# Expert results sent to a token-order table slot by slot, rotary tables made once and kept, first input tile and last output split, and the program's order laid anew

## What is computed

```python
xn = _layernorm(x, axis=-1)
x = x + _L0_attn_ref(xn, ...) + _L0_ffn_ref(xn, ...)
# attention: 16 query heads, 4 key/value heads, head size 128, causal
q = _layernorm(q, q_norm_w, q_norm_b); k = _layernorm(k, k_norm_w, k_norm_b)
q = _rope(q, cos, sin);                k = _rope(k, cos, sin)
attn = softmax(where(causal, q @ k.T / sqrt(D), -inf))
out = ((attn @ v) * sigmoid(gate)) @ w_o.T
# experts: 8, the two best of each token
top_vals, top_idx = jax.lax.top_k(x_flat @ w_router, 2)
probs = jax.nn.softmax(top_vals, axis=-1)
y = square(relu(x @ w_fc[e])) @ w_proj[e]        # for each expert e
out = sum over the token's two experts of probs * y
```

## Time and profile before

| | us |
|---|---|
| median of 3 runs | 1561.65 |
| lowest and highest | 1560.73, 1561.84 |
| profiled execution, its own time | 1561.02 |
| profiled execution, span of its instructions | 1559.2 |
| PE busy | 1508.5 (97%) |
| DVE busy | 1310.9 (84%) |
| ACT busy | 1154.7 (74%) |
| POOL busy | 523.9 (34%) |
| mean granted TensorE clock | 0.996 |

### The profile page before, as it was taken

The page is one execution under the profiler, slowest core; times in us unless marked ns, Lnnn a source line. Parts: engine busy times, 40 slices in busy tenths (PEclk is TensorE's granted clock), DMA queues, the critical chain, the costliest instruction groups (busy, mean ns, idle before and its releaser), DMA issues.

```text
span 1559.2 us, 29914 instructions
## 1 busy us (share of the span) xinstructions
PE 1508.5 (97%) x10589; PEld 1380.0 (89%) x10589; DVE 1310.9 (84%) x3011; ACT 1154.7 (74%) x3013; POOL 523.9 (34%) x726
## 2 busy tenths in 40 slices
PE   4999999999899999999999999999999999999998
PEld 3788999999899999999898999999998998899998
DVE  7999888787898888788789888887779988888875
ACT  3777777777778787787778777777777776776775
POOL 5544434320553222121046331221105535343200
PEclk9999999999999999999999999999999999999999
DMA  4400010001111000101211000110111101102000
GB/s 139 142 5 21 21 42 23 21 28 50 45 33 30 32 30 29 32 26 39 66 45 40 25 25 11 47 31 30 28 46 45 33 13 31 30 20 66 16 8 8
DMA packets 46646, 56.65 MB, mean 36 GB/s; under 512 B 4576, under 2 KB 43232, under 8 KB 46304
## 3 DMA queue, kind: packets, MB, share of 16 engines
q1 hardware_dynamic: 43424, 46.34, 9.5%
q0 software_dynamic: 3072, 8.39, 1.7%
HBM read 42.40 MB, written 18.35 MB: 39 GB/s over the span
## 4 chain that ended last, share of the span: by engine, by line
PE 74%; DVE 17%; ACT 5%; issue 2%; POOL 1%; DMA 1%; SPq 0%; DVEq 0%; ACTq 0%; POOLq 0%
PE bank L1286 39%; PE o_bank L1286 19%; PE pt_bank L1361 12%; DVE pT_lo L1219 3%; DVE neg_chunk_max L1205 2%; DVE t_same L1169 2%; DVE bank L1202 2%; PE bank L1339 1%; PE bank L1382 1%; DVE t_same L1165 1%; ACT probs L920 1%; DVE sumsq L1137 1%; DVE t_same L1153 1%; ACT gate L930 1%; ACT pT_hi L939 1%
## 5 line engine op out<-in xcount | busy, mean ns | idle before, releaser
L920 ACT ACTIVATE probs<-bank,neg_max 128x512 f32<-128x512 f32 (+3 forms) x640 | 399.8, 634 | 91.7 <-DVE neg_max L1212 57.6
L1219 DVE TENSOR_TENSOR pT_lo<-pt_bank,pT_hi 128x512 fp32r<-128x512 f32 (+1 forms) x576 | 368.7, 654 | 100.7 <-ACT pT_hi L939 96.8
L939 ACT ACTIVATE pT_hi<-pt_bank 128x512 fp32r<-128x512 f32 (+1 forms) x576 | 325.8, 578 | 131.3 <-PE pt_bank L1361 81.6
L1286 PE MATMUL o_bank<-pT_hi,v_hi 128*128 128x256 f32 x1088 | 333.7, 307 | 2.9 <-DVE pT_lo L1219 1.9
L1361 PE MATMUL pt_bank<-ident_f,probs 128*128 128x128 f32 x2176 | 315.2, 273 | 10.5 <-DVE pT_lo L1219 10.0
L785 POOL TENSOR_TENSOR t_swap<-qk_raw,table_swap 128x256 f32<-128x256 f32 (+1 forms) x256 | 135.4, 560 | 561.9 <-ACT t_same L889 560.9
L1286 PE MATMUL o_bank<-pT_hi,v_lo 128*128 128x256 f32 x1088 | 307.3, 282 | 0.0
L1286 PE MATMUL o_bank<-pT_lo,v_hi 128*128 128x256 f32 x1088 | 306.5, 282 | 0.0
L1205 DVE TENSOR_REDUCE neg_chunk_max<-bank 128x1 f32<-128x512 f32 (+1 forms) x384 | 244.8, 650 | 49.2 <-PE bank L1286 48.1
L1361 PEld LDWEIGHTS pt_bank<-ident_f,probs 128*128 128x128 f32 x2176 | 252.2, 140 | 36.0 <-DVE pT_lo L1219 13.5
L1286 PE MATMUL bank<-kT_hi,qT_hi 128*128 128x512 f32 (+3 forms) x640 | 244.0, 381 | 2.7 <-ACT probs L920 2.3
(11 more groups left out here) (163 smaller groups left out, 2974.6 us busy)
## 6 DMA issues: line engine op xcount, KB each, us to landing
rows<-xs SPq DMA_DIRECT2D x23, 256.0 KB, 2.7
expert_raw<-in_w_fc SPq DMA_DIRECT2D x23, 256.0 KB, 3.0
expert_raw<-in_w_proj SPq DMA_DIRECT2D x23, 256.0 KB, 2.7
yb<-rows SPq DMA_DIRECT2D x23, 256.0 KB, 2.1
xs<-in_x SPq DMA_DIRECT2D x11, 512.0 KB, 4.9
w_raw<-in_w_in SPq DMA_DIRECT2D x7, 640.0 KB, 4.3
angles<-in_cos_sin SPq DMA_DIRECT2D x64, 64.0 KB, 1.9
acc<-in_x SPq DMA_DIRECT2D x4, 512.0 KB, 8.3
```

The costliest lines, as they stand in the source:

```text
L920: act.activation(probs[:, u, h % 2, first:first + width], bank("scores", g, t, h, c)[:, 0:width], ACT.Exp, bias=neg_max[:, u, h % 2:h % 2 ...
L939: act.activation(pT_hi[:, n % PT_RING, 0:width], pt_bank[n % 2][:, 0:width], ACT.Copy)\
L1219: dve.tensor_tensor(pT_lo[:, n % PT_RING, 0:width], pt_bank[n % 2][:, 0:width], pT_hi[:, n % PT_RING, 0:width].bitcast(F32), ALU.subtract) ...
L1286: ins = pe.matmul(out_ap, s, m, start=(start and done == 1), stop=(stop and done == last))
```

## The change

Seven things are done together.

1. **Scatter of results.** Each row of `xs` gets two more columns, the number of the token's pair (2·token + j), scattered with the row; unused rows carry the number of a spare row. After `y_take`, POOL sends the slot's rows with two indirect DMAs (`y_place`) to the table `y_of` in token order, to the row numbers that DVE has made integers (`ids`). The second waits for the first, and the next `xs_load` waits for both. `y_store` and the 32 gathers are gone; after the last slot, SP reads `y_of` with 16 plain loads (`y_load`), through four buffers, and `comb` waits for these.
2. **Kept tables.** POOL makes the rotary tables only in group 0 (16 times, not 64). SP stores each to memory (384 KB) and loads it again in groups 1 to 3, alternately over `made_tables` and over the norm rows' place (48 loads of 384 KB); 48 loads of 64 KB of angles go.
3. **First tile.** x comes in parts of 1, 3, 4, 4 and 4 tiles; Q, K, V and the gate of tile 0 wait for the first alone. The router's products of tile 0 to 3 come later.
4. **Loads at the start.** The norm weights come as one load of rows already broadcast on the host's side; the router's weights are laid out by partition.
5. **Last tile.** Its `og`, `og_hi`, `og_lo` and `OUT` are done in two halves of two heads. `GT` and the first half of `OUT` stand ahead of the last products with V.
6. **Scatter order.** First all of j = 0, then all of j = 1.
7. **Order.** `BEGIN` and `DUE` have new numbers, with three shifts for each tile, and some costs of the plan are changed.

The core of the diff (the tables of numbers cut to a line):

```diff
-BEGIN = [26.59, 41.38, 29.62, 36.09, 25.65, 50.81, 47.59, 46.92, 64.18, 72.49, 75.23, 89.37, 102.35, 116.24,
+BEGIN = [4.36, 32.9, 50.6, 39.96, 9.9, 26.58, 41.54, 17.1, 36.65, 69.46, 20.35, 39.2, 39.91, 55.0, 87.1, 99.04,
...
+X_PARTS = ((0, 1), (1, 4), (4, 8), (8, 12), (12, 16))
...
+                if t >= 2:
+                    add("sp angles", ("angle_load", g, t), 0.45, [old(t2, "tables")], b0 + DUE["rope"] - 15, 64)
+                table = ("tables", g, t)
...
+                add("sp tables", ("table_store", t), 0.45, [table], 0, 384)
+            else:
+                table = ("table_load", g, t)
...
-            add("pool rope", ("swap", g, t), 2.0, [("kv_take", g, t), old(t1, "rope_b")], b0 + DUE["rope"])
+            add("pool rope", ("swap", g, t), 2.0, [("kv_take", g, t), table, old(t1, "rope_b")], b0 + DUE["rope"])
...
+                for p in range(HG // 2):
+                    add("dve out", ("og", g, t, p), 0.33, [("GT", g, t), ("o_take", g, t, p)], b2 + DUE["og"])
+                    add("act og", ("og_hi", g, t, p), 0.3, [("og", g, t, p), old(t1, "OUT")], b2 + DUE["og"])
+                    add("dve og", ("og_lo", g, t, p), 0.33, [("og_hi", g, t, p)], b2 + DUE["og"])
...
-        add("sp moe", ("y_store", m), 0.45, [("y_take", m)], at + 8, 256)
+        add("dve ids", ("ids", m), 0.1, [("xs_load", m)], at)
+        for k in range(2):
+            add("pool y", ("y_place", m, k), 1.27, [("y_take", m), ("ids", m), ("y_place", m, 0) if k else None], at + 8 + 6 * k, 2.0)
...
+        add("sp y", ("y_load", t), 0.45, [("y_place", NSLOT - 1, 1), ("comb", t - 4) if t >= 4 else None], at + 20 + 3 * t, 256)
...
-                    for i, v in enumerate((q_w, k_w)):
-                        sp.dma_start(ln_w[:, i, :], v.partition_broadcast(P)).then_inc(tables_in, 16)
-                    for i, v in enumerate((q_b, k_b)):
-                        sp.dma_start(ln_b[:, i, :], v.partition_broadcast(P)).then_inc(tables_in, 16)
+                    sp.dma_start(norm_rows[:, 0:2], norm_in).then_inc(tables_in, 16)
...
+                elif kind == "table_load":
+                    g, t = a
+                    n = g * T + t
+                    w.wait_ge(tables_kept, 16 * T)
...
+                elif kind == "y_place":
+                    m, k = a
+                    w.wait_ge(ids_done, m + 1)
+                    w.wait_ge(y_taken, m + 1)
+
+                    w.wait_ge(y_placed, 32 * m + 16 * k)
+                    pool.indirect_dma_start(y_of, bass.IndirectOffsetOnAxis(row_to[:, k:k + 1], 0), rows[:, k, 0:C], None)\
+                        .then_inc(y_placed, 16)
...
+                elif kind == "ids":
+                    m = a[0]
+                    w.wait_ge(xs_in, 16 * (m + 1))
+                    dve.tensor_copy(row_to[:], rows[:, :, C]).then_inc(ids_done, 1)
```

More of the change, by code:

```diff
@@ L157, in old @@
         return (kind, *tile, *rest) if tile is not None else None
-    for q in range(4):
-        add("sp", ("x_load", q), 0.5, [], 0, 512)
-        if q == 0:
+    for n, (first, last) in enumerate(X_PARTS):
+        add("sp", ("x_load", n), 0.5, [], 0, 128 * (last - first))
+        if n == 0:
             add("sp", ("ident_load",), 0.5, [], 0, 64)
@@ L199, in program_steps @@
         add("sp fill", ("fill", k), 0.45, [("tables", 0, 1 + k // 3)], 30 + k, 512)
-    for t in range(T):
-        for j in range(2):
-            add("pool sc", ("scatter", t, j), 1.27, [("route", ROUTE_PLACE), ("fill", FILLS - 1), ("turn_probs", *prob_steps[SCATTER_AT + SCATTER_EVERY * (2 * t + j)])],
-                DUE["scatter"], 2.0)
+    for j in range(2):
+        for t in range(T):
+            add("pool sc", ("scatter", t, j), 1.27, [("route", ROUTE_PLACE), ("fill", FILLS - 1), ("row_ids", j),
+                ("turn_probs", *prob_steps[SCATTER_AT + SCATTER_EVERY * (T * j + t)])], DUE["scatter"], 2.0)
+        add("act ids", ("row_ids", j), 0.25, [("scatter", T - 1, 0)] if j else [("ident_load",)], 20)
     for g in range(G):
@@ L1010, in _ @@
                 elif kind == "stats":
-                    q = a[0]
-                    w.wait_ge(x_in[q], 16)
-                    for t in range(4 * q, 4 * q + 4):
+                    first, last = X_PARTS[a[0]]
+                    w.wait_ge(x_in[a[0]], 16)
+                    for t in range(first, last):
                         dve.bn_stats(x_stats[:, t, :], acc[:, t, :]).then_inc(stats_done, 1)
-                    for t in range(4 * q, 4 * q + 4):
+                    for t in range(first, last):
                         w.wait_ge(stats_done, t + 1)
@@ L1018, in _ @@
                 elif kind == "norm":
-                    q = a[0]
-                    w.wait_ge(rstd_x_done, 2 * q + 2)
-                    w.wait_ge(means_done, 4 * q + 4)
-                    for t in range(4 * q, 4 * q + 4):
-                        dve.tensor_scalar(xn[:, t, :], acc[:, t, :], x_mv[:, t, 0:1], x_rstd[:, t:t + 1],
+                    first, last = X_PARTS[a[0]]
+                    w.wait_ge(rstd_x_done, 2 * a[0] + 2)
+                    w.wait_ge(means_done, last)
+                    for t in range(first, last):
+                        dve.tensor_scalar(xn[:, t, 0:C], acc[:, t, :], x_mv[:, t, 0:1], x_rstd[:, t:t + 1],
                                           ALU.subtract, ALU.mult).then_inc(xn_done, 1)
@@ L1388, in _ @@
                     w.wait_ge(wo_lo_done, g + 1)
[L1389 to L1391 removed]
+                    heads = range(HG) if (g, t) != LAST_TILE else range(HG // 2)
+                    three(bank("OUT", g, t)[:, 0:C], [(ogT_hi[:, h * P:(h + 1) * P], ogT_lo[:, h * P:(h + 1) * P]) for h in heads],
+                          [(wo_hi[:, h, :], wo_lo[:, h, :]) for h in heads], stop=(g, t) != LAST_TILE).then_inc(filled, 1)
+                elif kind == "OUT_rest":
+                    g, t = LAST_TILE
+                    w.wait_ge(og_lo_done, g * T + t + 2)
+                    heads = range(HG // 2, HG)
+                    three(bank("OUT", g, t)[:, 0:C], [(ogT_hi[:, h * P:(h + 1) * P], ogT_lo[:, h * P:(h + 1) * P]) for h in heads],
+                          [(wo_hi[:, h, :], wo_lo[:, h, :]) for h in heads], start=False).then_inc(last_out, 1)
                 elif kind == "XS":
```

316 lines of the change are left out of this document (182 added, 134 removed), and 32 rows, old and new, of the table BEGIN.

## The result

| | us |
|---|---|
| kernel before, median | 1561.19 |
| changed kernel, median of 4 runs | 1536.28 (1535.15 to 1537.13) |
| ratio, with its 95% interval | 0.9844 (0.9832 to 0.9856) |
| changed kernel, profiled execution: own time, span | 1536.08, 1534.3 |

The change is 24.9 us faster.

The account below looks back on a forecast made before the run. PE was taken as the bound, busy 1508.5 of 1559.2 us, leaving 50.7 us to win. Start -3, end -1 and middle -4, slots at nothing, summed to -8 us: 1553.6 us, range 1545 to 1563.

Parts of the forecast that it names:

- The start: First 20 us and what follows: shorter waits and sooner DVE work give -3 us, at best -5, at worst 0.
- three waits for loads: At the start: ACT's wait for broadcast constants, late-landing broadcast rows, and a first x of 512 KB, all to shrink or go.
- The end: After the last product with V: halves cut 5.3 us to 3.0, net -1.2; `comb` loading DVE adds 0.2; together -1.
- The middle: From 100 to 1540 us: -3 from order, -1.5 from POOL's silence, +0.5 for `ids`; -4, ends -10 and +7.
- POOL's silence: In the middle: with table work gone from POOL, DVE's two-input instructions run shorter, bringing PE 1.5 us.
- its transfers were hidden before: Said of the results' scatter: it changes nothing at all on PE's path.
- Order: In the middle: the new order of everything, priced from DVE lists against PE lists, gives -3 us.
- The slots: Way from Y to the next XS grows from 5.4 to 8.3 us; costed at nothing, 1.2 us spare in the tightest.
- POOL becomes a link of the slots: Rival: busy POOL and late `y_take` make PE stand for XS in some ten slots; 1569 us, chance 0.10.
- The middle goes much further: Rival: POOL's tables were behind the late `pT_lo` too, so the middle loses 12 us; 1545.6 us, chance 0.14.
- Handed back on DVE: Rival: PE's waits shift rather than go, middle and end together at 0 or +2; about 1560 us, chance 0.20.
- descriptors starved: Rival: indirect DMAs of each pair take the longer issue, 1.664 us, making tight slots late; 1560.6 us, chance 0.04.

Follow-up runs that it names:

- remade: Changed kernel, its lists kept, with POOL making the rotary tables again in all four groups and none stored or loaded: 1565.9 us.
- start_loads: Changed kernel with the first part of x as one 512 KB load again and the norm rows broadcast by four loads: 1537.0 us.
- new_start: The change's mechanisms on the old kernel's lists, results stored by plain DMA, with the changed kernel's lists for the first 70 us planned: 1549.3 us.
- no_comb: Changed kernel without the 32 instructions that add the experts' rows and without their loads: 1536.4 us.
- kept_only: Kernel before with kept tables alone, same lists on PE, ACT and DVE: 1556.6 us, against 1561.2.
- remade_plain: `remade` with the scatter of results replaced by SP's one plain DMA per slot: 1540.7 us.
- place_double: Changed kernel with each of a slot's two scatters sent twice, same rows to the same places: 1654.4 us.

## The prediction against the result, step by step

**What bounds the kernel: right.** All that changed was PE's lost time. Of the 25.0 us, adding the parts one after the other on the way from before gives: kept tables 4.3, gathers gone 6.7, the start 7.7, the rest of the middle 5.7, the end 0.6. It is one way of several: taken back from the changed kernel, the tables alone are 29.6.

**The start: -3 forecast, -7.5 measured.** Its signs were right: first weight product at 9.12 (about 10), the constants 11.09 against 15.59, Q at 14.46 (about 15), first rotated turn at 28.89 (about 29.5), DVE unused for 5.6 of the first 20 us (about 5.4). PE busy came to 6.65, not 7.5 to 9: in this execution Q's products ran 0.23 us apart, where I had taken the 0.43 us of the earlier trace rows. That is chance: of nine traces with the same lists up to there, four have 6.65 to 6.94 us, and five 7.29 to 7.80, in `remade` with Q's products 0.43 us apart. The step that failed is the cause, and with it the size. I priced three waits for loads; `start_loads` gives the first tile's and the norm rows' share back and costs 0.7 us. What gained is the order: `new_start` has 5.5 us from the lists alone. In the new lists the router's products of two quarters no longer stand ahead of the first rotation and the first scores; that this is what counts in them is read from the traces and not tested by itself. I had counted DVE's sooner use (2.8 us), and not that PE's list lost two blocks on the way to the first scores. A part may also be DVE's shorter instructions, which I looked for in the middle only. The 16 `xn`, before and after:

```profile
L1023 DVE TENSOR_SCALAR xn<-acc,probs 128x256 f32<-128x256 f32 x16 | 8.0, 565 | 0.7 <-POOL probs L747 0.7
```

```profile
L1121 DVE TENSOR_SCALAR xn<-acc,probs 128x256 f32<-128x256 f32 x16 | 6.3, 462 | 1.1 <-POOL probs L839 1.1
```

**The end: -1 forecast, -1.4 measured.** 3.0 us from the last take to the last add, as worked out. The load of `comb` was 0.2 in the sum and is too small to measure by `no_comb`; DVE is busy 34.6 of the last 40 us, under the 90% that I had given as a sign.

**The middle: -4 forecast, -16.1 measured.** Three terms failed. *Kept tables*: 1.5 us for POOL's silence, with the rotation's 3.6 as a bound that I then left out; 5.3 by `kept_only`. PE's waits for `t_same` only went from 3.6 to 2.9 us there, so which of the two it was stays open. *Gathers*: nothing, measured 6.8. The step is the last line on the rivals, "its transfers were hidden before". It took the gathers as free because PE waited for no transfer of theirs. What the runs show in its place are PE's own signals, up to 3.3 us late while the gathers run, with DVE and then PE standing for them. A part of the cost was in the earlier trace rows, under the name of `pT_lo`. *Order*: 3 us, from pricing the DVE lists against the PE lists; about 5.7 by the table, with the scatter in it, and inside the bounds of -10 and +7.

**The slots: right, and closer to the edge than its weight in the text.** The way was 8.3 us in the forecast. Measured are 0.8 from `y_take`'s end to the first scatter, 2.8 to the second, 2.4 to the load's issue (medians of 22) and 2.6 until it lands: 8.6. The tightest slot has 10.0 from ACT's end to XS, and 3.4 us is the least from a load's issue to its XS, so 0.8 to spare where I had 1.2. But the cost is nothing only in this order and with kept tables: in the old order it is 46 us, with POOL's tables 25 (`remade` against `remade_plain`). My rival "POOL becomes a link of the slots" is the mechanism of `remade`; its price of 0.7 us a slot was far too low, since its terms were single handovers and not a whole tile's work on POOL. Its sum was off as well: 0.8 us in each of 23 slots on top of 1553.6 is 1572 and not 1569, and the forecast gain of 8 us is eaten from 0.35 us a slot on, not from 0.7. And in pricing the moved load I named DVE at `ids` as the one behind, and missed the load that stands behind it on SP.

**The rivals.** "The middle goes much further" (1545.6, 0.14) was the nearest, too small, and for another reason than its own: with kept tables alone PE still waited 8.3 us for `pT_lo`, 9.0 before. "Handed back on DVE" and "descriptors starved" didn't come: the longest of 46 scatters took 1.497 us to issue, their median 1.046:

```profile
L903 POOL DMA_INDIRECT y_of<-rows,row_to x46: 962/1046/1497, 395.4 to 1477.7; - x46
```

The range failed because the ends of the terms (-5, -1.2 and -10, which make 1545.5) were not the ends of what was unpriced. The gathers had no term and so no end.

## What to carry to other kernels

Price a removed step as carefully as an added one, and don't stop at who waits for its result: the gathers held nobody up by name, and cost 6.8 us. Where an engine stands although what it needs ended long before, look at what else was running. When a transfer gets longer, walk down the list of the queue that now waits for it; an independent load one place behind can cost more than the transfer itself, and moving it costs nothing. Where an order was searched together with a mechanism, the parts can't be added up: undoing the kept tables measured 29.6 us beside the scatter, 2.0 without it and 5.3 in the old kernel.

## What the runs showed of the hardware

DVE's instructions came in two lengths. In the kernel before, the 512-column `ogT_lo`, which reads two tiles of SBUF, took 0.682 us on average in the 48 cases in which POOL ran none of its multiplications for the tables and the `swap`, and 1.026 (up to 1.244) in the 16 that met one; `pj_lo` 0.681 and 0.973. `pT_lo` of the same size, which reads one tile of PSUM, took 0.685 and 0.681. So the mean excess of 0.09 us in the earlier trace rows was a third of a microsecond in a quarter of the cases. `xn`, with one tile of SBUF in and one out, did it too, 0.408 and 0.686. Indirect DMAs on POOL lengthened none of them (`ogT_lo` 0.688 in two cases, and 0.685 in nine of the changed kernel). The Trainium skill, in GPSIMD Engine Reference, Specifications, has DVE instructions with two SBUF inputs or in a two-port mode contend with GpSimd; the trace agrees for two SBUF inputs. Which mode `xn` ran in, no row tells.

PE's clock was granted 0.90 in the first 20 us and 0.92 from 20 to 100, against 1.00 and 0.98 in the earlier trace rows: from 17 to 22 us, in which PE stands (6.1 us before 23.66), the granted clock was 0.50, the lower of its two levels. It is not fixed by the lists: `remade`, with the same ones, had 1.00 and 0.98. The start is faster nonetheless. I had looked at PE's own spacing there, and not at when the clock would be granted.

PE's signals came late while gathers ran back to back. I compared the moment of each event by which PE tells the others of a product, some 2320 in a trace, with the last product before it that gives one, so that what comes out is the least that it can be late. Up to PE's last product, 15 in the kernel before and 14 in `kept_only` came at least 0.35 us late, up to 2.7, all in or just behind the four runs of gathers issued some 1.3 us apart. None did in the 16 traces without gathers, not even with 46 scatters of results (92 in `place_double`), issued 2.7 us apart or more.
